# Retained values with tokens on partitions: row sums as a product column, division on VectorE, transposes back on PE

## What is computed

```python
k, q, v = jnp.split(x @ wkqv, 3, axis=-1)
qkt = jnp.einsum("bid,bjd->bij", q, k) / jnp.sqrt(jnp.float32(d))
row_norm = 1.0 + jnp.sqrt(jnp.arange(s, dtype=x.dtype))[None, :, None]
r = jnp.tril(qkt) / row_norm
denom = jnp.clip(jnp.abs(r.sum(-1, keepdims=True)), 1.0, None)
r = jnp.einsum("bij,bjd->bid", r / denom, v)
m = r @ w1 + b1
a, gate = jnp.split(m, 2, axis=-1)
m = _groupnorm1(a * jax.nn.silu(gate) @ w2 + b2, gg, gb)
y = m + h
f = jax.nn.gelu(y @ wf1 + bf1_, approximate=False) @ wf2 + bf2_
h = _layernorm(f + y, lg, lb)
```

## Time and profile before

| | before |
|---|---|
| median of 3 runs | 2643.9 us (2637.84 to 2644.37) |
| profiled execution | 2644.7 us, span 2642.9 us |
| PE busy in the span | 2493.1 us (94%) |
| DVE busy | 1739.8 us (66%) |
| ACT busy | 1333.7 us (50%) |
| POOL busy | 1362.8 us (52%) |
| mean granted clock of PE | 0.978 |

### The profile page before, as it was taken

How to read it: one execution, slowest core, us unless ns; L and a number is a source line. 1 busy time by engine, 2 the same in 40 slices (tenths; PEclk the granted TensorE clock), 3 DMA queues, 4 the chain that set the end, 5 groups by cost and what they waited for, 6 DMA issues and landing times. The chain is left out here.

```text
span 2642.9 us, 35142 instructions
## 1 busy us (share of the span) xinstructions
PE 2493.1 (94%) x11574; PEld 2052.7 (78%) x11574; DVE 1739.8 (66%) x2906; ACT 1333.7 (50%) x2288; POOL 1362.8 (52%) x1258
## 2 busy tenths in 40 slices
PE   7999999999999999984899999999999999999997
PEld 5788778887888778862677778878888788888886
DVE  2677777778777877764667774656646556455445
ACT  3465655565555655543455554444444444444443
POOL 2244554444444554445577785455654546554544
PEclk9999999999999999996999999999999999999999
DMA  5100001001200010004565554443344434344441
GB/s 160 61 32 32 32 24 63 19 31 32 72 32 32 32 40 32 24 16 140 187 211 181 171 202 179 168 156 143 146 179 159 165 122 166 140 169 164 144 165 68
DMA packets 99962, 283.54 MB, mean 107 GB/s; under 512 B 6384, under 2 KB 76416, under 8 KB 83456
## 3 DMA queue, kind: packets, MB, share of 16 engines
q1 hardware_dynamic: 99712, 282.01, 30.7%
q10 hardware_dynamic: 128, 0.03, 0.0%
HBM read 212.42 MB, written 69.60 MB: 107 GB/s over the span
## 5 line engine op out<-in xcount | busy, mean ns | idle before, releaser
L1333 POOL TENSOR_TENSOR hid_lo<-full,hid_hi 128x512 fp32r<-128x512 f32 x384 | 498.4, 1311 | 569.4 <-ACT full L1436 459.4
L1614 DVE SCALAR_TENSOR_TENSOR full<-m_ps,bias_cols,sum 128x512 f32<-128x512 f32 x384 | 288.2, 750 | 215.5 <-PE m_ps L1715 201.5
L1713 PE MATMUL m_ps<-hid_hi,m_w 128*128 128x512 f32 x1024 | 403.5, 394 | 0.2 <-POOL hid_lo L1333 0.2
L1715 PE MATMUL m_ps<-hid_hi,m_w 128*128 128x512 f32 x1024 | 401.4, 392 | 0.0
L1714 PE MATMUL m_ps<-hid_lo,m_w 128*128 128x512 f32 x1024 | 401.3, 392 | 0.0
L1713 PE MATMUL m_ps<-m_t_hi,m_w 128*128 128x512 f32 x896 | 355.5, 397 | 27.8 <-DVE full L1614 17.5
L1714 PE MATMUL m_ps<-m_t_lo,m_w 128*128 128x512 f32 x896 | 351.6, 392 | 0.0
L1715 PE MATMUL m_ps<-m_t_hi,m_w 128*128 128x512 f32 x896 | 351.6, 392 | 0.0
L1433 ACT ACTIVATE hid_hi<-m_ps,bias_cols 128x512 fp32r<-128x512 f32 x128 | 88.3, 690 | 495.3 <-PE m_ps L1715 495.3
L322 POOL TENSOR_TENSOR pf_lo<-tmp,pf_hi 128x512 fp32r<-128x512 f32 x128 | 161.6, 1296 | 168.0 <-ACT pf_hi L498 168.0
L1440 ACT ACTIVATE hid_hi<-full 128x512 fp32r<-128x512 f32 x256 | 161.9, 632 | 164.0 <-DVE full L1614 163.8
(11 more groups left out here) (195 smaller groups left out, 5664.1 us busy)
## 6 DMA issues: line engine op xcount, KB each, us to landing
m_w<-prepared SPq DMA_DIRECT2D x96, 1408.0 KB, 6.0
prepared<-m_w SPq DMA_DIRECT2D x32, 1408.0 KB, 5.8
h_store<-h_out SPq DMA_DIRECT2D x32, 512.0 KB, 3.2
m_raw<-in_L_ffn_W SPq DMA_DIRECT2D x64, 256.0 KB, 6.4
gate_bc<-gate_rows SPq DMA_DIRECT2D x32, 512.0 KB, 6.7
h_in<-h_store SPq DMA_DIRECT2D x24, 512.0 KB, 4.3
h_in<-in_L_attn_x SPq DMA_DIRECT2D x8, 512.0 KB, 5.1
raw<-in_L_attn_Wf SPq DMA_DIRECT2D x8, 512.0 KB, 8.1
```

Source lines behind the costliest of these rows:

```text
L1333: nc.gpsimd.tensor_tensor(out=hid_lo[:, k, :], in0=full[:, k, :], in1=f32(hid_hi[:, k, :]), op=ALU.subtract).then_inc(hid_ready, 1)
L1614: nc.vector.scalar_tensor_tensor(out=full[:, k, :], in0=src, scalar=b1_col(e, 2 * fp + BLOCK_ROW[k]), in1=other[:, :], op0=ALU.add, op1=AL ...
L1713: nc.tensor.matmul(out, w[0], x[0], start=first, stop=False, skip_group_check=True)
L1715: return nc.tensor.matmul(out, w[1], x[0], start=False, stop=last, skip_group_check=True)
```

## The change

The retention has its operands turned round. The masked scores are stationary and h moves, so that the result has tokens on partitions and features along the row. h gets two more columns, one in the high half and zero in the low half, so each matmul is 258 wide and the row sum of each token stands in column 256 of its own row (the second column keeps the width even). For block k of 128 tokens, k+1 blocks are added up: 10 products of three matmuls, 30 in all. The eight matmuls with ones are gone.

`divide` on DVE takes the place of `divisor`, `invert` and `scaled`. In three groups (blocks 0 and 1, then 2, then 3) it forms the divisor and reciprocal on 128x2 or 128x1 elements, each step waiting until the one before has landed, and multiplies each block of 128x256 out of PSUM into `r_tok`, which lies in the tile y. `transpose_r` on PE then makes 8 transposes of 128x128 back to features on partitions, blocks 0 and 1 when both are there, 2 and 3 each when there; ACT and DVE split the result as before. The gate reads its product from PSUM, and so does `gated`.

The order on PE: in slot A the up projection of B is cut in two, with the transposes between the halves; in slot B they stand between the two halves of the down projection of A. In the first pass ACT empties the second fold ahead of `high_r`.

```diff
         ident = sb("ident", [P, P])
-        ones_r = sb("ones_r", [P, P], F32R)
         mean_w = sb("mean_w", [P, P])
         neg_half = sb("neg_half", [P, TB])
-        floor = sb("floor", [P, S])
+        floor = sb("floor", [P, TB])
         const_rows = sb("const_rows", [L * LC, P])
...
         h_out = slot_tiles("h_out", [P, TB, D])
-        h_sp = split_tiles("h", [P, TB, D])
+        h_sp = split_tiles("h", [P, TB, D + 2])
         hT_sp = split_tiles("hT", [P, DC, S])
...
         z = slot_tiles("z", [P, TB, D])
-        inv = [t[:, 0, :] for t in y]
+        r_tok = [t[:, :, :].rearrange("p c (k d) -> p (c k) d", d=D) for t in y]
+        den = slot_tiles("den", [P, 2, TB])
         warm = sb("warm", [P, 1])
...
                                     base=0, pattern=[[-1, P]], channel_multiplier=1).then_inc(pool_consts, 1)
-            nc.gpsimd.memset(f32(ones_r[:, :]), 1.0).then_inc(pool_consts, 1)
+            for s in range(SLOTS):
+                nc.gpsimd.memset(f32(h_sp[s][0][:, :, D:D + 2]), 1.0).then_inc(pool_consts, 1)
+                nc.gpsimd.memset(f32(h_sp[s][1][:, :, D:D + 2]), 0.0).then_inc(pool_consts, 1)
             nc.gpsimd.memset(neg_half[:, :], -0.5).then_inc(pool_consts, 1)
             nc.gpsimd.memset(mean_w[:, :], 1.0 / (P * DC)).then_inc(pool_consts, 1)
-            pool.wait_ge(pool_consts, 5)
+            pool.wait_ge(pool_consts, 8)
...
                 for c in range(DC):
-                    act.wait_ge(r_psum[s], at.base + 2 * c + 2)
+                    act.wait_ge(rT_psum[s], at.base + 2 * c + 2)
                     nc.scalar.activation(ry_sp[s][0][:, c, :], bank(s, 2 + c), ACT.Copy).then_inc(r_hi[s], 2)
...
                 act.wait_ge(lc_ready[s], at.layer + 1)
-                act.wait_ge(gate_scaled[s], at.base + 2 * c + 2)
-                nc.scalar.activation(tmp[s][:, 2 + c, :], tmp[s][:, 2 + c, :], ACT.Silu,
+                act.wait_ge(m_psum[s], at.base + 2 * c + 1)
+                nc.scalar.activation(tmp[s][:, 2 + c, :], bank(s, GATE[c]), ACT.Silu,
                                      bias=lc_bm1[s][:, DC + c:DC + c + 1]).then_inc(gate_ready[s], 2)
...
                 else:
+                    empty_fold(2)
                     high_r(A_, now)
-                    empty_fold(2)
                 load_table(ACT.Silu)
...
-            def divisor(s, at):
+            def divide(s, at):
                 base = at.it * SCALE_CHAIN
-                dve.wait_ge(rowsum_psum[s], at.base + U)
-                landed(nc.vector.tensor_tensor(out=y[s][:, 1, :], in0=bank(s, 0), in1=floor[:, :], op=ALU.max), scale_done[s], base + 1)
-                nc.vector.scalar_tensor_tensor(out=y[s][:, 1, :], in0=bank(s, 0), scalar=-1.0, in1=y[s][:, 1, :],
-                                               op0=ALU.mult, op1=ALU.max).then_inc(scale_done[s], 1)
-
-            def invert(s, at):
-                base = at.it * SCALE_CHAIN
-                dve.wait_ge(scale_done[s], base + 2)
-                nc.vector.reciprocal(inv[s], y[s][:, 1, :]).then_inc(scale_done[s], 1)
-
-            def scaled(s, at, c, banks, out, which, done):
-
-                dve.wait_ge(m_psum[s], at.base + 2 * c + which)
-                dve.wait_ge(scale_done[s], at.it * SCALE_CHAIN + SCALE_CHAIN)
-                nc.vector.tensor_tensor(out=tmp[s][:, out + c, :], in0=bank(s, banks[c]), in1=inv[s], op=ALU.mult).then_inc(done[s], 2)
+                for n, (k, width) in enumerate(((0, 2), (2, 1), (3, 1))):
+                    r = (2 + k) % 4
+                    sums = ps[:, 4 * s + r:4 * s + r + width, D]
+                    dve.wait_ge(r_psum[s], at.base + k + width)
+                    landed(nc.vector.tensor_tensor(out=den[s][:, 0, k:k + width], in0=sums, in1=floor[:, k:k + width], op=ALU.max),
+                           scale_done[s], base + 3 * n + 1)
+                    landed(nc.vector.scalar_tensor_tensor(out=den[s][:, 0, k:k + width], in0=sums, scalar=-1.0, in1=den[s][:, 0, k:k + width],
+                                                          op0=ALU.mult, op1=ALU.max), scale_done[s], base + 3 * n + 2)
+                    landed(nc.vector.reciprocal(den[s][:, 1, k:k + width], den[s][:, 0, k:k + width]), scale_done[s], base + 3 * n + 3)
+                    for c in range(k, k + width):
+                        nc.vector.tensor_scalar(r_tok[s][:, c, :], score_bank(s, c)[:, 0:D], den[s][:, 1, c:c + 1], None,
+                                                ALU.mult).then_inc(r_kept[s], 1)
             def gated(s, at, c):
-                dve.wait_ge(value_scaled[s], at.base + 2 * c + 2)
+                dve.wait_ge(m_psum[s], at.base + 2 * c + 2)
                 dve.wait_ge(gate_ready[s], at.base + 2 * c + 2)
                 nc.vector.scalar_tensor_tensor(
-                    out=tmp[s][:, c, :], in0=tmp[s][:, c, :], scalar=lc_bm1[s][:, c:c + 1],
+                    out=tmp[s][:, c, :], in0=bank(s, VALUE[c]), scalar=lc_bm1[s][:, c:c + 1],
                     in1=tmp[s][:, 2 + c, :], op0=ALU.add, op1=ALU.mult).then_inc(u_ready[s], 2)
...
-                scaled(s, at, 0, GATE, 2, 1, gate_scaled)
-                scaled(s, at, 0, VALUE, 0, 2, value_scaled)
+                gated(s, at, 0)
                 meanwhile(0)
-                gated(s, at, 0)
-                scaled(s, at, 1, GATE, 2, 1, gate_scaled)
                 low_u(s, at, 0)
-                scaled(s, at, 1, VALUE, 0, 2, value_scaled)
                 gated(s, at, 1)
...
                     groupnorm_out(B_, before)
-                divisor(A_, now)
+                divide(A_, now)
                 low_r(A_, now)
-                invert(A_, now)
                 if seam:
...
                     layernorm_var(B_, before)
-                divisor(B_, now)
+                divide(B_, now)
                 low_r(B_, now)
-                invert(B_, now)
...
             def retain(s, at):
-                def weighted_h(b):
-                    q = slice(LO[b], S)
+                pe.wait_ge(h_lo[s], at.base + U)
+                for k in range(TB):
+                    pe.wait_ge(p_masked[s], at.base + k + 1)
+                    for b in range(k + 1):
+                        ins = mm3(score_bank(s, k)[:, 0:D + 2], both(pf_sp[s], ALL, b, cols(k)), both(h_sp[s], ALL, b), b == 0, b == k)
+                    ins.then_inc(r_psum[s], 1)
+
+            def transpose_r(s, at):
+                for k in range(TB):
+                    pe.wait_ge(r_kept[s], at.base + max(k + 1, DC))
                     for c in range(DC):
-
-                        pe.wait_ge(p_masked[s], at.base + max(b, c) + 1)
-                        ins = mm3(bank(s, 2 + c)[:, q], both(h_sp[s], ALL, b, cols(c)), both(pf_sp[s], ALL, b, q),
-                                  b == 0, b == TB - 1)
-                        if b == TB - 1:
-                            ins.then_inc(r_psum[s], 2)
-
-                pe.wait_ge(h_lo[s], at.base + U)
-                weighted_h(0)
-                weighted_h(1)
-                for b in range(TB):
-                    q = slice(LO[b], S)
-                    pe.wait_ge(p_masked[s], at.base + max(b, 2) + 1)
-                    for half in range(2):
-                        ins = nc.tensor.matmul(bank(s, 0)[:, q], ones_r[:, :], pf_sp[s][half][:, b, q],
-                                               start=b == 0 and half == 0, stop=b == TB - 1 and half == 1,
-                                               skip_group_check=True)
-                ins.then_inc(rowsum_psum[s], U)
-                weighted_h(2)
-                weighted_h(3)
+                        ins = nc.tensor.transpose(bank(s, 2 + c)[:, cols(k)], r_tok[s][:, k, cols(c)], ident[:, :])
+                        if k == TB - 1:
+                            ins.then_inc(rT_psum[s], 2)
...
                 for r, n in ((GATE[0], DC), (VALUE[0], 0), (GATE[1], DC + 1), (VALUE[1], 1)):
-                    if r == 0:
-                        pe.wait_ge(scale_done[s], at.it * SCALE_CHAIN + 2)
                     for k in range(DC):
...
-            def up_projection(s, at):
+            def up_projection(s, at, chunks=range(DC)):
                 w = weight("f1", DC)
                 pe.wait_ge(w_lo, split_count("f1", at.layer))
-                for k in range(DC):
+                for k in chunks:
                     pe.wait_ge(y_lo[s], at.base + 2 * k + 2)
...
                 if before:
-                    up_projection(B_, before)
+                    up_projection(B_, before, (0,))
                 else:
                     fold(2)
+                transpose_r(A_, now)
+                if before:
+                    up_projection(B_, before, (1,))
                 gated_projection(A_, now)
...
                 retain(B_, now)
-                for c in range(DC):
-                    down_projection(A_, now, c)
+                down_projection(A_, now, 0)
+                transpose_r(B_, now)
+                down_projection(A_, now, 1)
...
```

(2 more changed lines are left out.)

## The result

The changed kernel takes 2627.8 us in the median of 5 runs (2622.7 to 2632.7), the kernel before, run beside it, 2643.9 us (2637.8 to 2645.6). The ratio over all runs is 0.9949 (the two medians alone give 0.9939), with a 95% interval of 0.9927 to 0.9970. So the change makes the kernel faster by 0.5%; the prediction said 2658 us, slower. The execution profiled took 2631.6 us (span 2629.8), against 2644.7 us (span 2642.9) before: 13.1 us less.

What follows compares the result with a forecast made beforehand. PE, busy 97.5% of a pass, was taken as the bound. Instructions and waits +6.8 us and clock falls +8 gave +14.8 on the profiled 2644.7 us; against the 2643.9 median the forecast was 2658 us, range 2636 to 2677.

Steps and rivals of the forecast that it cites:

- `divide`: DVE's division per slot: nine small steps at 0.27 us and four products at 0.40, 4.1 us in all.
- the clock: PE's granted clock halves behind slot A's new wait in 5 of 15 passes, 1.6 us each: +8 us.
- the first pass: No pair before it, so the copy and subtraction after `high_r` stand open before the gated projection: +1 us.
- the end: After the last pair most of PE's waits for `tu_lo` go: -2.6 us.
- Slot B, -0.6 us: PE instructions: 30 matmuls 3.55 us plus transposes 0.88 replace a 5.03 us retention; the division is covered.
- The `tu_lo` wait goes, -1.4 us: PE's 1.24 us wait in slot B's output projection goes; with the restart worth 1.4 us a pass.
- Slot A behind S, +2.67 us: After slot A's first retention matmul starts (S), PE waits for the division; the gated projection starts 2.7 us later.
- The rival that priced it low: Division takes 2.9 us, deciding from about 3.4 downward; plain pass -0.55 us, faster at 2633 us; chance 0.17.
- Slot A was to lose 1.25 us: Slot A's net per pass: 1.4 us won on the `tu_lo` wait, 2.67 lost waiting for the division.
- A plain pass, +0.65 us: Slot A +1.25 and slot B -0.6 us; twelve such passes give +7.8 us.
- seam: Three seams, where the `tu_lo` wait that goes is up to 1.6 us: about +0.2 us each, +0.6.
- the signs by which I was to be wrong: A's gated projection under 13 us after S, clock never or always falling, or slot B's transposes waiting.

Runs made afterwards that it cites:

- e6: Kernel after the change with 384 bytes in front of `hT`, weights-to-streamed distance 128 modulo 512 bytes as before: 2639.4 us, ratio 0.9994.
- e8: Kernel after the change with a slot's four row sums inverted in one go, three waits instead of nine: 2613.4 us, ratio 0.9895.
- e12: Kernel after the change with 64 bytes in front of `floor` and 320 in front of `hT`, distance 64: 2630.8 us in one execution.
- e2: Kernel after the change with a 32-byte tile in front of `floor`, moving all tiles behind it: 2627.1 us, ratio 0.9951.
- e10: Kernel after the change with 384 bytes in front of `hT` and 128 more in front of `tmp`: 2637.7 us in one execution.
- e11: Kernel after the change with 320 bytes in front of `hT`, distance 64: 2633.6 us in one execution.
- e5: Kernel before the change with 128 bytes in front of `hT`, distance 256 modulo 512: 2637.5 us, ratio 0.9984.
- e1: Kernel before the change with a 32-byte tile in front of `floor`, moving all tiles behind it: 2641.1 us, ratio 1.0003.
- e3: Kernel before the change with hT, tu, ry and pf moved by 32 bytes, what lies behind by 64: 2646.8 us, ratio 1.0023.
- e4: Kernel after the change with slot A's transposes in the middle of the second half of the up projection: 2615.9 us, ratio 0.9903.
- e9: Kernel after the change with slot A's transposes moved into the up projection's second half and row sums inverted in one go: 2603.0 us, ratio 0.9847.

## Why the prediction was wrong

The range (2636 to 2677) did not hold 2627.8, and the sign was wrong. Four terms of the sum failed, and one thing had no term: `divide` (4.1 us, measured 3.4), the clock (+8 us, measured nothing net), the first pass (+1, measured -5.9), the end (-2.6, measured +4.7), and the place of the tiles in SBUF, which made every 512-wide matmul against the weights 5 ns faster. By its own steps:

- **Slot B, -0.6 us: right.** To read it without the cadence I take e6: its slot B half (from slot B's first transpose to slot A's next) is 68.69 - 38.46 = 30.2 us, against 30.85 before, so -0.6. The retention took 3.62 us (3.55 said), the transposes have their cover.
- **The `tu_lo` wait goes, -1.4 us: right.** 18.0 us in 15 passes became 1.8.
- **Slot A behind S, +2.67 us: +1.92.** The order of events was right to about a tenth (retention, first half at S + 4.69, division from S + 6.65); the size of `divide` was wrong. It is 3.4 us and not 4.1: 0.19 us a small step instead of 0.27, which I had taken from the step after one with a read of another tile in the earlier trace rows, while the first pair of those rows, at 0.20, was the better match. The rival that priced it low set its threshold at "about 3.4 us", and this is where it landed; but that threshold does not follow from the prediction's own sum, which gives -4 us at 3.4 and needs about 3.1 to come out under 2636. The rival came true in its sign and not by its mechanism. Slot A was to lose 1.25 us; e6 lost 0.46 (38.49 against 38.03), which is 1.92 - 1.4.
- **A plain pass, +0.65 us: -0.2 at equal cadence** (68.70 in e6 against 68.9). Most of the difference is the 0.7 us of `divide`, and e8 shows from the other side that a microsecond taken off the division is a microsecond of the pass.
- **The clock, +8 us: wrong in size.** I took a fall in 5 of 15 passes behind the new wait; there was one. In windows of 2 us the changed kernel's clock falls at 362, 406 and 642 us between the first pass and the last, 13.6 us at half speed in all; the kernel before has the same 13.6 us (368, 654 and 938). The falls at 362 and 642 lie at seams. The one at 406 comes right behind the three waits for the division in a plain pass, where I had looked for it (timeline of PE, then windows):

```profile
405.91 0.41 PE L935 MATMUL ps<-ident,y 128*128 128x128 f32 x2 [0.62 <-DVE y L672]
```

```profile
406.60:410.00 3.40, 3.40 (x10) 2.62 (x9) 1.29 (x2) 2.70 (x5) 0.00 (x0) 0.50 0.03 7
```

  That pass takes 69.63 us instead of 67.95, so a fall costs 1.7 us, as priced. e12 has the same fall in the same pass (405.9 us); e2, e6, e10 and e11, with the same three waits, have none outside the seams. That is 2 falls in some 90 passes. A single wait of nearly that length is not safe either: in e5 PE waited 1.79 us for `tu_lo` once, and the clock fell behind it, at 398.8 us.
- **The first pass, +1 us: -5.9.** I had priced the chain and not the clock. The windows view of the same 80 us, in the kernel before and then after:

```profile
20.00:100.00 80.00, 69.16 (x303) 53.72 (x303) 30.52 (x51) 39.27 (x72) 23.88 (x28) 0.89 0.37 119
```

```profile
20.00:100.00 80.00, 69.61 (x343) 54.66 (x343) 30.68 (x72) 39.51 (x73) 23.51 (x28) 0.96 0.36 119
```

  The windows of 2 us give 17.0 us at half speed in the kernel before, 6.8 in the one after: 10.2 us less, worth 5.1. The fall at 64 us, behind a wait for an operands' load (3.04 us before, 1.11 after), is in every profile of the unchanged program (before, e1, e3, e5), and none of the changed one has it. Why that load's wait is shorter was not looked for. e1, the kernel before with its tiles moved, had 10.2 us of half clock and a first pass of 82.2 us.
- **The end, -2.6 us: +4.7.** The two waits for `tu_lo` behind 1160 us (3.2 us in all) are all but gone (0.2 us left), as laid out. But the clock is at half for 20 us longer between the last pass's start and the end, and the prediction had no clock term there.
- **Not in the sum at all: the cadence.** -0.76 us a plain pass by e6 against after (68.70 to 67.94), 10.9 us from the first pass's start to the last one's (1065.4 to 1054.6 us), of which 1.7 are 3.4 us more at half clock in e6. In ratios it is 0.9994 against 0.9949, about 12 us, which is nearly all of the gain measured. The diff showed it, in one line that got no price: `h_sp`, two columns more in each of four tiles, 4 x 32 = 128 bytes more between the weights and the streamed tiles. (`ones_r` and `floor`, which the prediction did list, lie in front of both and move them together, which e1 and e2 show to be worth nothing.) I asked what the tiles cost to fill, and not what stands behind them in SBUF.

The profiled execution was forecast at +14.8 us and came at -13.1, 27.9 apart. Cadence 11.4 (15 x 0.76), `divide` 10.5 (15 x 0.7), clock 8, first pass 6.9, less 7.3 for the end, make 29.5, which is 1.6 us more than there is; the seams and the single fall of the clock are left aside in it.

With `divide` at 3.4 us and no falls of the clock my sum would have come to about -4 us (plain pass -0.05, seam -0.5, the first pass and the end as they stood), no change, and no change is what e6 measured (ratio 0.9994). That agreement is partly luck: in e6's profile the first pass is 5.7 us shorter than before and the stretch from the last pass's start 4.5 us longer, and these two errors nearly cancel. None of the signs by which I was to be wrong came either (the gated projection started at S + 13.2, the clock fell at times, slot B's transposes did not wait): none of them looked at instructions that the change leaves alone.

**What stays open.** Why the distance matters is not shown. The timeline of the kernel before shows PE loading the next weights beside the matmul that runs:

```profile
724.33 0.47 PE L865 MATMUL ps<-ry_hi,w_hi 128*128 128x512 f32 x1 [0.23 <-DVE ry_lo L624]
724.40 0.19 PEld L866 LDWEIGHTS ps<-ry_lo,w_hi 128*128 128x128 f32 x1
```

Both read SBUF at that time, and that fits a cost that depends on the distance of the two and on nothing else that was moved; but no run here tells the load from the stream. Nor is the curve known beyond the distances tried: 0 (0.2282 us), 64 (0.2299), 128 (0.2326 and 0.2331), 160 (0.2345), 256 (0.2281 and 0.2285). The pads also moved `pf` against `h`, which is streamed past it in the retention: the 258-wide matmuls start 0.122 us apart in the changed kernel and 0.121 in e6 and e10. That is the other way and under 0.1 us a pass; no run was made for it.

## What to carry to other kernels

When a change adds, drops or resizes an SBUF tile, one between the weights and what PE streams above all, compare the start-to-start time of matmuls that it does not touch before you credit its code with anything; and where PE is the bound, put the weights and what it streams at a distance that is a multiple of 256 bytes (0 and 256 modulo 512 are what was tried here). Price a chain of small dependent VectorE steps from the nearest pair of the same kind in the trace, then count what an order with fewer waits would save: here five small steps with three waits, in place of nine with nine, were worth 1.0 us a pass, about as much as the plain pass gained from the change and its side effect together. The wait that was left behind a moved piece of work went away here when that piece was moved a little further into the matmuls that follow it, with something left behind it to cover the copies (e4, e9).

## What the runs showed of the hardware

- Back-to-back 512-wide matmuls of fp32 operands against the weights' tiles start 0.228 us apart when the weights and the streamed tile lie 0 or 256 bytes apart (modulo 512), 0.230 at 64, 0.233 at 128 and 0.2345 at 160; moving both by 32 or 64 bytes together changes nothing (e1 and e2, e11 against e12).
- Dependent VectorE steps on 1 or 2 elements a partition, each with a wait on the one before, start 0.19 us apart (duration 0.15 to 0.17); independent ones in e8, two in 0.22 us together, start some 0.06 us apart. The Trainium skill ("VectorE: DVE Perf Modes", The DRAIN you can't avoid) says that a semaphore after each of a row of copies costs nothing extra. For a step that waits on its predecessor these rows differ, and they decide.
- The granted clock fell to half (1.2 GHz) behind three waits of 0.3 to 0.6 us with transposes between them in 2 of some 90 passes (the changed kernel and e12, at 406 us), and once behind a single wait of 1.79 us (e5, at 398.8 us). Such a fall in a plain pass cost 1.7 us.
